# Latent stage of a four-layer kernel: middle parts cast and low parts subtracted once per group, the rests in a row, statistics in front of them

## What is computed

```
xn  = layernorm(x)                      # over the 256 values of a token
c_q = xn @ W_dq ;  c_kv = xn @ W_dkv    # 256 -> 64 each
Q = c_q @ W_uq ;  K = c_kv @ W_uk ;  V = c_kv @ W_uv   # 64 -> 16 heads x 16
```

## Time and profile before

| what | value |
|---|---|
| median of 3 runs (lowest to highest) | 2794.38 us (2794.3 to 2799.74) |
| the profiled execution: device time / span in the trace | 2794.65 / 2792.9 us |
| PE, DVE, ACT, POOL busy over the span | 88%, 79%, 63%, 20% |
| latent stage, in the trace | 47 to 220 us |
| in it busy: PE, DVE, ACT, POOL | 137.5, 145.2, 82.6, 77.5 of 173 us |
| in it: share of the 16 DMA engines, rate | 0.81, 250 GB/s |

### The profile page before, as it was taken

The page is one execution under the profiler, slowest core; times in us unless marked ns, Lnnn a source line. Parts: engine busy times, 40 slices in busy tenths (PEclk is TensorE's granted clock), DMA queues, the critical chain, the costliest instruction groups (busy, mean ns, idle before and its releaser), DMA issues. The chain is left out here.

```text
span 2792.9 us, 57214 instructions
## 1 busy us (share of the span) xinstructions
PE 2454.0 (88%) x15239; PEld 1155.9 (41%) x15239; DVE 2199.0 (79%) x5740; ACT 1767.6 (63%) x2700; POOL 562.1 (20%) x644
## 2 busy tenths in 40 slices
PE   5888999999999999578999997994999999996756
PEld 2442333333333333254666664663333333333645
DVE  6887999899999898286777767996666676666968
ACT  2452666666666666316777755884778788873546
POOL 1543111111111111240000000223222222222300
PEclk8996999999999999898999998997999999998879
DMA  6985353535454543360000002556866776664503
GB/s 187 287 280 122 77 108 81 105 84 103 86 102 87 102 87 83 85 182 1 0 0 0 0 0 68 188 188 184 162 144 142 148 145 144 141 138 118 149 8 117
DMA packets 224106, 309.46 MB, mean 111 GB/s; under 512 B 32416, under 2 KB 170352, under 8 KB 211952
## 3 DMA queue, kind: packets, MB, share of 16 engines
q1 hardware_dynamic: 223616, 307.47, 45.6%
q10 hardware_dynamic: 432, 1.31, 0.2%
HBM read 181.29 MB, written 126.88 MB: 110 GB/s over the span
## 5 line engine op out<-in xcount | busy, mean ns | idle before, releaser
L947 ACT ACTIVATE a_p<-psum 128x1024 f32<-128x1024 f32 (+1 forms) x640 | 567.3, 942 | 303.9 <-PE psum L1045 303.7
L947 ACT ACTIVATE b_p<-psum 128x512 f32<-128x512 f32 (+2 forms) x640 | 444.2, 750 | 145.1 <-PE psum L1045 142.0
L999 DVE CUSTOM_DVE_ANT_0 a_dump<-psum,a_bias 128x128 bf16<-128x128 f32 (+3 forms) x1024 | 446.3, 488 | 56.5 <-PE psum L1034 48.1
L997 DVE TENSOR_REDUCE a_peak<-psum 128x1 f32<-128x512 f32 x512 | 334.7, 688 | 27.6 <-PE psum L1034 25.0
L976 DVE COPY b_twin<-psum 128x512 f32<-128x512 f32 (+1 forms) x320 | 204.0, 637 | 164.5 <-PE psum L1045 161.2
L1045 PE MATMUL psum<-b_qs,b_ks 96*128 96x512 bf16 (+3 forms) x1536 | 307.1, 330 | 28.6 <-DMA b_vs<-values 28.6
L1061 PE MATMUL psum<-b_p,b_vs 128*32 128x512 f32 (+3 forms) x3072 | 314.7, 497 | 6.3 <-POOL b_p L919 6.2
L919 POOL TENSOR_SCALAR_AFFINE_SELECT a_p<-a_p 128x512 f32<-128x512 f32 x256 | 162.3, 634 | 753.7 <-ACT a_p L947 742.0
L1034 PE MATMUL psum<-a_ks,a_qs 96*128 96x128 bf16 (+2 forms) x1008 | 277.4, 333 | 19.3 <-DVE a_peak L999 13.9
L919 POOL TENSOR_SCALAR_AFFINE_SELECT b_p<-b_p 128x512 f32<-128x512 f32 x256 | 159.3, 634 | 441.1 <-DVE b_p L979 429.8
L1045 PE MATMUL psum<-a_qs,a_ks 98*128 98x512 bf16 x1008 | 234.2, 328 | 13.0 <-DMA a_qs<-a_rows 10.8
(11 more groups left out here) (197 smaller groups left out, 3647.3 us busy)
## 6 DMA issues: line engine op xcount, KB each, us to landing
qk_parts<-l_parts SPq DMA_DIRECT2D x96, 256.0 KB, 3.2
qk_parts<-g_parts SPq DMA_DIRECT2D x96, 256.0 KB, 2.6
values<-l_vx SPq DMA_DIRECT2D x64, 256.0 KB, 3.4
sums<-a_osb SPq DMA_DIRECT2D x64, 256.0 KB, 2.1
m_num<-sums SPq DMA_DIRECT2D x64, 256.0 KB, 3.8
m_inv<-reciprocals SPq DMA_DIRECT2D x64, 256.0 KB, 4.6
values<-g_vx SPq DMA_DIRECT2D x64, 256.0 KB, 3.0
sums<-b_osb SPq DMA_DIRECT2D x64, 256.0 KB, 2.1
```

The lines of the kernel that those rows point to most:

```text
L947: act.activation(p[s % SLOTS][:, 2 * k:2 * k + heads, cols], m.psum[:, at:at + heads, cols], ACT.Exp if softmax else ACT.Square, scale=z.D ...
L997: last = dve.tensor_reduce(dst, piece, AX.X, ALU.max)
L999: last = dve.tensor_tensor_reduce(dump[c % SRING][:, at:at + w], piece, bias[:, 512 - w:], 1.0, NEG, ALU.add, ALU.max, dst)
```

## The change

DVE's `norm` is cut in two: `measure` (the wait for x and the statistics) and `norm` (reciprocal and normalised rows). `split` keeps only the four subtractions, now one behind another. A new `middle` waits for the last of them and casts all four banks in one instruction of 2048 columns. The order in the loop becomes measure(n+2), split(n), norm(n+2), middle(n); ahead of the loop it is measure and norm of groups 0 and 1 as before; behind it split and middle of groups 14 and 15. POOL makes all four low parts in one instruction behind one wait. SP's wait for the middle parts is adapted to the new count. PE's and ACT's programs are as before.

```diff
-                sp.wait_ge(mid_done, 4 * n + 4)
+                sp.wait_ge(mid_done, n + 1)
...
-            def norm(i, u):
-                n = 2 * i + u
-                tiles = of_group(z, m.x, n)
+            def measure(i, u):
+                n = 2 * i + u
                 if isinstance(i, int) and i == 0:
                     dve.wait_ge(m.x_first, 16)
                 else:
                     dve.wait_ge(m.x_rest, 16 * (z.B - 1))
-                statistics(m, dve, tiles, raw[u], mv[u], raw_done, mv_ready, n)
+                statistics(m, dve, of_group(z, m.x, n), raw[u], mv[u], raw_done, mv_ready, n)
+
+            def norm(i, u):
+                n = 2 * i + u
                 inverse(dve, sd[u], rs[u], sd_ready, rs_ready, n)
                 dve.wait_ge(turned, n + 1)
-                normalise(dve, xn[u], tiles, mv[u], rs[u]).then_inc(xn_ready, 1)
+                normalise(dve, xn[u], of_group(z, m.x, n), mv[u], rs[u]).then_inc(xn_ready, 1)
...
                     dve.tensor_tensor(rest[u][:, j, :], m.bank[QK0 + j][:, :], parts[u][:, 0, j, :],
                                       ALU.subtract).then_inc(rest_done, 1)
-                    dve.wait_ge(rest_done, 4 * n + j + 5)
-                    dve.tensor_copy(parts[u][:, 1, j, :], rest[u][:, j, :]).then_inc(mid_done, 1)
-
-            staggered(dve, GROUPS, norm, split)
+
+            def middle(i, u):
+                n = 2 * i + u
+                dve.wait_ge(rest_done, 4 * n + 8)
+                dve.tensor_copy(parts[u][:, 1, :, :], rest[u][:, :, :]).then_inc(mid_done, 1)
+
+            for u in range(2):
+                measure(0, u)
+                norm(0, u)
+            with dve.Fori(0, GROUPS // 2 - 1) as i:
+                for u in range(2):
+                    measure(i + 1, u)
+                    split(i, u)
+                    norm(i + 1, u)
+                    middle(i, u)
+            for u in range(2):
+                split(GROUPS // 2 - 1, u)
+                middle(GROUPS // 2 - 1, u)
...
-                    for j in range(4):
-                        wait_alone(pool, mid_done, 4 * n + j + 1, m.alone)
-                        last = pool.tensor_tensor(parts[u][:, 2, j, :], rest[u][:, j, :], parts[u][:, 1, j, :],
-                                                  ALU.subtract)
-                    last.then_inc(low_done, 1)
+                    wait_alone(pool, mid_done, n + 1, m.alone)
+                    pool.tensor_tensor(parts[u][:, 2, :, :], rest[u][:, :, :], parts[u][:, 1, :, :], ALU.subtract
+                                       ).then_inc(low_done, 1)
```

## The result

| | before | after |
|---|---|---|
| median of the runs shown together | 2794.34 us | 2833.44 us (2832.45 to 2834.59) |
| ratio, 95% interval | | 1.014 [1.012, 1.016] |
| span of the profiled execution | 2792.9 us | 2832.6 us |
| `heads` of group 0 to `heads` of group 14 (14 cycles) | 136.35 us | 171.17 us |
| `heads` of group 14 to the attention's first product | 23.55 us | 23.18 us |

The time moved the way that was forecast, but by 39.1 us in place of 21.1, and out of the range. Of the 39.7 us between the two spans 34.8 are in the 14 cycles of the latent stage, -0.4 at its end and 5.3 behind it.

The account below looks back on a forecast made before the run. A serial loop through the normalised rows was taken to bound the latent stage at 11.2 us a cycle: +20.4, plus 0.7 for stores, is +21.1 on 2794.65; less 0.3 for the median, 2815.5 us, range 2808 to 2828.

Parts of the forecast that it names:

- What bounds the stage: Latent stage before: PE's own round of 8.95 us bounds eight of 14 cycles, DVE five, and one is a stall.
- The sum of the loop: Latent stage, heads through normalised rows and turn to the next heads: 11.14 us a cycle, taken as 11.2.
- the term of +20.4: Latent stage: 14 cycles of 11.2 us, 156.8 against 136.35, so 20.4 us slower.
- So 2.2 us should keep 2.4 GHz: PE's wait ahead of each turn in the latent stage: 2.2 us of idling should not lower its clock.
- Rival 2: Latent stage: PE's clock falls in every cycle, turn, values and down double, +3.6 us each, time about 2866; chance 0.05.
- no stretch of this trace does so: Said of the skill's loop that starts cold each time: the trace before shows no such stretch.
- They delay neither: Latent stage: POOL's 4.08 us subtraction runs beside statistics, before the next rows or cast, and delays neither.
- The wait for stores: Latent stage, ACT waiting near group 6 for group 4's stores: 0 to 1.5 us stay, taken as +0.7.
- The tail at nothing: End of the latent stage: group 15's new low parts are hidden by 0.8 us behind SP's last stores, costing nothing.
- Later stages shifted and not changed: Stages behind the latent stage: listed as a sign that the forecast is right; no cost was given to them.
- Rival 1: Latent stage: locked casts bind, not the loop; cycles fall to 8.95 us, time 2790.8 or 2783.3; chance 0.06.
- its upper case: Latent stage: loop plus whole stall, one to three slow-clock cycles, or late cast and statistics; 2822 to 2830; chance 0.13.

Follow-up runs that it names:

- the last kernel: Against the kernel before: rests in a row behind the normalised rows, four casts back to back, four subtractions, seven first loads spread over the groups; 2785.38 us, ratio 0.9971.
- the kernel with PE's wait filled: The changed kernel with two extra products of 0.86 us each on PE between values(n, 0) and turn(n+2); 2823.88 us, ratio 1.0111.
- With POOL started: The changed kernel with one small subtraction of 32 columns on POOL ahead of its loop; 2833.24 us, ratio 1.0140.
- the kernel without them: The changed kernel with two extra PE products where PE waits and a small POOL subtraction ahead of its loop; 2820.76 us, ratio 1.0098.
- the spread loads alone: The kernel before with the seven first loads issued one at a time behind the stores of seven groups; 2790.59 us, ratio 0.9990.

## Why the prediction was wrong, point by point

- **What bounds the stage** held. PE's own round of 8.95 us is what the last kernel reaches.
- **The sum of the loop** held to 0.01: 11.14 against 11.15. PE waits 2.05 us and the rows come at +6.61 (68.88 - 62.27), forecast 2.2 and +6.62. The rounding up to 11.2 was for nothing; the term of +20.4 measured 19.8.
- **"So 2.2 us should keep 2.4 GHz"** is the first step that failed. It compared the one wait with a longer one that had kept the clock, in a stage whose cycles are filled otherwise. In after the granted clock falls in every second cycle, 0.68 over the stretch against 1.00, and costs 1.67 us each time, 9.9 in all, and 2.7 more in the long cycle; the kernel with PE's wait filled shows no such cycle. Rival 2 had the mechanism with a chance of 0.05, and a price of 3.6 a cycle in all 14. What came is about half of the cycles and half of the price, since `turn` keeps the high clock (1.09 us) and the clock is back before `down` ends. The Trainium skill's case of a loop that waits in each turn (TensorE: Matmul & The Clock Gate, "HAM oscillation — how this bites in real kernels") is what the trace shows, in every second turn and not in each; the trace decides. The prediction set the case aside with "no stretch of this trace does so". None starts at the low clock in every turn, but one comes near, and it was passed over: in the second mixing stage of before, in cycles of about 7.4 us, the transposes run now at half clock and now at full, behind waits of 0.2 to 2.8 us, and the granted clock is 0.88 over 70 us (0.50 over the first transposes shown). This stage, and not the one of the earlier trace rows, was the nearest row for a wait that comes back in each turn.

```profile
2581.22 1.96 PE L185 MATMUL psum<-ident,m_xn 128*128 128x128 f32 x8 [2.63 <-ACT m_xn L1294]
...
2623.60 1.09 PE L185 MATMUL psum<-ident,m_xn 128*128 128x128 f32 x8 [2.75 <-ACT m_xn L1294]
```

```profile
2580.00:2650.00 70.00, 52.14 (x232) 43.04 (x233) 64.73 (x249) 37.38 (x76) 23.52 (x10) 0.88 0.52 151
2581.20:2583.20 2.00, 1.98 (x9) 1.99 (x10) 1.85 (x9) 0.05 (x1) 2.00 (x1) 0.50 0.96 248
```

- **"They delay neither"**, of POOL's subtraction, is the second. It was reasoned for the steady state. The trace of before had POOL's first subtraction start at 72.74 with 22.8 us of "issue" ahead of it, 7.5 us after the first cast; the prediction has no term for that delay. With the cast later the delay puts it on the rows of group 3: 5.2 us (16.38 - 11.15), 2.6 by the rows' lateness and 2.7 by the clock behind it. With POOL started the cycle is one of the regular ones of 12.82, and with PE's wait filled as well one of 11.14.
- **The wait for stores**, 0.7 out of 0 to 1.5: in after it is absent, hidden by the slower cycles; in the kernel without them it is 1.24 (12.38 - 11.14). The term's bounds were right for the cycle that it was worked out with.
- **The tail at nothing** held: 23.18 us against 23.55.
- **"Later stages shifted and not changed"** is the third that failed, 5.3 us in the span: the attention fell into its slower rhythm. That it could depend on DVE's program in another stage no row of before showed.
- **Rival 1** lost as forecast: the rows are on the path. But with the rows in front the batched kernel still takes 0.22% more time than before, and a gain beyond the 0.1% of the spread loads alone is there only with the rests in a row, the loads spread and DVE's program at its old length.

Together 19.8 (14 x 11.15 - 136.35) + 9.9 + 5.2 - 0.4 + 5.3 = 39.8, against 39.7 between the spans. The range ended at 2828 since its upper case took these effects one at a time, the clock for one to three cycles, and the third not at all.

## What to carry to other kernels

When a step is moved behind others on its engine, write down who waits for its result and close the loop: here the time of one cycle could be summed from the old trace to a hundredth, though the engine in question had become less busy. A new wait of PE in each turn of a loop is priced twice, at its length and at the clock behind it; look in the old trace for a stage that already waits in each turn. A long instruction on POOL is a lock on DVE's casts and scalar operations. Place it beside DVE's rests and statistics, which kept their 0.69 and 1.4 us beside it here, and look at its first use by itself. Before a gain is hoped for, look at what is next in line; here stores behind a burst of loads would have eaten it.

## What was not expected of the hardware

- POOL's first subtraction in the stage starts 7.4 us late (7.5 in before); with a small one of the same kind ahead of it, which is late in its place, the next starts after 0.18 us.
- Casts on DVE that follow each other directly mostly keep POOL out: 0.42 us each in the median against 0.98 with a rest between them.
- The clock fell with waits of 2.05 and 0.86 us in a cycle of 11.15, in every second cycle, and was back within the cycle.
- Three tiny instructions more or fewer in DVE's program of one stage change each unit of a later stage by 0.2 us of 28, by which of two instructions a POOL instruction holds.
- The last stage's products run over 77.8 us in before and in after, and over 80.3 to 82.2 in four of the kernels tried. The granted clock falls once or twice more in these; why is open.
